# K's bias moved from a matmul to VectorE, and pieces of the order moved, in a fused attention and mixture-of-experts kernel on one core

## The chip, the core and the metric

The kernel runs on one NeuronCore of a Trainium2 chip. The core has TensorE (matmuls and transposes, which write into eight PSUM banks of 128 x 512 floats), VectorE, ScalarE and GpSimd (elementwise work), and SyncE, whose queue issues most of the DMAs. Each engine takes its instructions strictly in its own order; between engines only semaphores order the work. The metric is the device time of one execution in microseconds, lower is better.

## The reference, cut to what matters

For x of shape 2 x 1024 x 512, with a modulation (sa, ca, ga, sb, cb, gb) made from c:

```
h = layernorm(x) * (1 + ca) + sa
Xn = layernorm(h) * gamma + beta
Q, K, V = split(Xn @ W_in + b_in)
K, V = rotary(K), rotary(V)                  # first 256 of 512 columns
A = 0.5 * sum_over_tokens(K/|K| * V/|V|) + 0.5
x = x + ga * ((A * Q) @ W_out + b_out + h)
h = layernorm(x) * (1 + cb) + sb
scores = softmax(h @ gate_w); top 2 of 8 experts
routed = sum over the 2 experts: weight * (silu(h @ w_gate_e) * (h @ w_up_e)) @ w_down_e
shared = (silu(h @ sw_gate) * (h @ sw_up)) @ sw_down     # 704 inner columns
x = x + gb * (routed + shared)
```

## The kernel before, in words

All large products are made of three matmuls (`product3`): each float32 factor is split into a high part, rounded to the matmul's format (ScalarE copies it: the functions that end in `_hi`), and the rest (VectorE subtracts: `_lo`); high x high, high x rest and rest x high are summed in a bank. The 2048 tokens are 16 tiles of 128 (NT = 16, eight for each of the two rows of x). The order of each engine is written out by hand.

**First phase, K and V** (loop over t = 0 to 15). TensorE: K of tile t (`kv_matmul(t, 0)`, 12 matmuls and one that adds the bias row), transposes of tile t + 1, V of tile t, small pieces named in SLOT_A and SLOT_B (tables of cosines, q's transposes, the modulation "mod", the vector "a0"), and `weighted_sums(t - 1)`. The bias row is kept in two rows of `bk` and added by a matmul with a column of two ones, L1866. Banks 2 and 4 hold K, 3 and 5 V. ScalarE: `v_square(t - 1)`, `k_row(t)` (copies K into `ksb`), `tokens_hi(t + 1)`, `k_square(t)` (sum of squares), table reads, `normed(t + 2)`, and for t = 10 to 13 `scaled_q`. VectorE: `products(t - 1)` (L1174, L1175 and the rotary product L1187), `modulated(t + 2)` (L1138 to L1145), `tokens_lo(t + 1)` (L1149), `x_statistics(t + 3)` (L1120 to L1122), parts of `wo` for t = 8 and 9, `scaled_q_lo` for t = 10 to 13 (L1230). GpSimd makes the powers (L593, L598). K's tile t needs `tokens_lo(t)`; the transposes of t + 1 need `normed(t + 1)`.

**Middle.** `m_first`, `h_matmul` and `m_second` fold A into the output matrix (mw), `y_bias` and `y_bias_rows` make one bias row `bh` from bank 7, and `spread_mod(1)` brings the shift sb of the second norm to all partitions (`bc_s`).

**Second phase, y** (loop over t). TensorE: `y_matmul(t)`, a bias matmul L2165, `m_second`, parts of the gate's logits, `transposes2(t - 2)`, and after the tiles in Y_CHUNKS one chunk of the shared expert's gate and up for group 0 (a chunk is 128 of the 704 inner columns, a group four tiles; chunk n needs `s_mul` of chunk n - 1 because all chunks of this phase use banks 4 and 5). VectorE: `second_rows` (L1338), statistics, `residual_part`, `tokens2_lo` (L1357), `ffn_rows` (L1350, L1352), for t = 6 four `m_block_late` and four `m_block_lo_late`, and `s_mul` (L1365) and `s_lo` (L1373) of the chunks.

**Third phase, shared expert and slots.** For g = 0 to 3 `shared_gate_up(g)` and `shared_down(g)`: down tiles t take banks 6, 7, 0 in turn and in the last group 6, 7. VectorE scales and adds the rows (`shared_rows`, L1472 and L1474, which release the bank by `s_row`), counts the slots of the tokens (`row_entries`, `slots`, `entry_experts`), and builds 32 one-hot matrices, three at a time (`one_hots`), which TensorE sums in the order of `slot_sums`. `columns()` reads the sum, GpSimd then gathers the tokens of experts 0 and 1 (L667), and `turn_rows` transposes them in steps (0 to 4) at the places in TURN_AT, between the tiles of `shared_down(3)`.

**Fourth phase, experts.** Pairs of experts in a loop, TensorE full, gathers and scatters on GpSimd.

Of the kernel before, what the change touches and what calls it, by code (L numbers as in the profile page):

```python
# [23 lines left out]
P = 128  # L24
# [40 lines left out]
Y_CHUNKS = {6: 0, 9: 1, 12: 2, 14: 3}  # L65
# [8 lines left out]
def build(nc, X, W_in, b_in, W_out, b_out, gamma, beta, gate_w, w_gate, w_up, w_down,  # L74
# [10 lines left out]
    with ctx:  # L85
# [27 lines left out]
        with ExitStack() as a_phase:  # L113
# [10 lines left out]
            arow = al("arow", [P, B, ROT])  # L124
            bk = al("bk", [P, D], F32R)
# [166 lines left out]
        def s_down_bank(t):  # L292

            return bank[(6, 7, 0)[t % 3] if t < NT - GT else (6, 7)[t % 2]]
# [64 lines left out]
        TURN_AT = [(0, 0, 1), (0, NS - 1, 0), (0, NS - 1, 1), (1, 0, 2), (1, 0, 3)]  # L359
# [49 lines left out]
        def _(sp):  # L409
# [60 lines left out]
            sp.wait_ge(bias_mm, 2)  # L470
# [26 lines left out]
            sp.wait_ge(h32_ready, 1)  # L497
# [208 lines left out]
        def _(act):  # L706
# [18 lines left out]
            def bias_row_hi(i):  # L725

                act.wait_ge(bias_mm, i + 1)
                nc.scalar.activation((bk, bv)[i][:, :], bank[(W_BANK, MISC_BANK)[i]][:, :], ACT.Copy).then_inc(bias_hi, 1)
# [16 lines left out]
            def k_row(t):  # L745

                act.wait_ge(k_mm, t + 1)
                if t >= 2:
                    act.wait_ge(multiplied, t - 1)
                nc.scalar.activation(ksb[:, t % 2, :], bank[K_BANKS[t % 2]][:, :], ACT.Copy).then_inc(k_copied, 1)  # L750

            def k_square(t):
                if t:
                    act.wait_ge(v_sq, t)
                nc.scalar.activation(junk[:, :], bank[K_BANKS[t % 2]][:, :], ACT.Square,
                                     accum_out=nrm[:, t, 0:1]).then_inc(k_sq, 1)
# [57 lines left out]
            normed(1)  # L814
            bias_row_hi(1)
# [3 lines left out]
            for t in range(NT):  # L819
# [7 lines left out]
                k_row(t)  # L827
# [90 lines left out]
            for k in range(1, DC):  # L918
                scaled_q(1, k)
            m_block_hi(0, 3)  # L920
            shared_in_hi(0)
            act.wait_ge(h32_ready, 1)
            nc.scalar.activation(bh[:, :], junk[:, :], ACT.Copy).then_inc(bh_hi, 1)
            shared_in_hi(1)
# [4 lines left out]
            for t in range(NT):  # L929
# [9 lines left out]
                if t == NB - 2:  # L939
                    for i in range(DC):  # L940
                        m_block_hi_late(i)
                if t in Y_CHUNKS:
                    s_silu_of(0, Y_CHUNKS[t])
                if t - 1 in Y_CHUNKS:
                    s_hi_of(0, Y_CHUNKS[t - 1])

            def shared(g):
                for m in range((DC, 2, 0, 0)[g], NS):
# [3 lines left out]
                    if not g and m == DC:  # L952
                        tokens2_hi(NT - 2)
                        tokens2_hi(NT - 1)
                        shared_down_hi(0)
                s_hi_of(g, NS - 1)
                if not g:
                    read_parts(NG - 1)
                    shared_down_hi(1)
# [133 lines left out]
        def _(dve):  # L1093
# [64 lines left out]
            def bias_rows(i):  # L1158

                dve.wait_ge(bias_hi, i + 1)  # L1160
                dve.scalar_tensor_tensor((bk, bv)[i][:, :], (bk, bv)[i][:, :].bitcast(F32), nodd[:, :],
                                         bank[(W_BANK, MISC_BANK)[i]][:, :], ALU.mult, ALU.add).then_inc(bias_ready, 1)

# [89 lines left out]
            weights_lo(0)  # L1253
            tokens_lo(0)
# [7 lines left out]
            x_statistics(2)  # L1262
            for t in range(NT):
# [7 lines left out]
                if 1 <= t < NT - 1:  # L1271
                    tokens_lo(t + 1)
                if t + 3 < NT:
# [27 lines left out]
            def y_factors():  # L1301

                for b in range(B):
                    at = slice(b * Q4, (b + 1) * Q4)
                    dve.tensor_copy(comb_ga[at, :], bc_ga[at, b, :])
                    link(dve.tensor_tensor(comb_s[at, :], bc_s[at, b, :], bc_ga[at, b, :], ALU.mult))

            def y_bias():
# [3 lines left out]
                link(dve.tensor_tensor(junk[:, :], bank[H_BANK][:, :], bout[:, :], ALU.add))  # L1312
                link(dve.tensor_tensor(junk[0:half, :], junk[0:half, :], bank[H_BANK][half:P, :], ALU.add))
# [121 lines left out]
            def shared(g):  # L1435
                for m in range((DC, 2, 0, 0)[g], NS):
# [3 lines left out]
                    if not g and m == DC:  # L1440
                        tokens2_lo(NT - 2)
                        tokens2_lo(NT - 1)
                        shared_down_lo(0)
# [157 lines left out]
            def slots():  # L1601

                link(dve.scalar_tensor_tensor(flat(rr), flat(low), float(CAP - GN), flat(rr), ALU.mult, ALU.add))
# [193 lines left out]
        def _(pe):  # L1797
# [54 lines left out]
            def kv_matmul(t, i):  # L1852

                to = bank[(K_BANKS, V_BANKS)[i][t % 2]][:, :]
                if t >= 2:
                    pe.wait_ge((k_sq, v_sq)[i], t - 1)
                if i == 0:
                    pe.wait_ge(t_lo, t + 1)
                for k in range(DC):
                    if t == 0:  # L1860
                        pe.wait_ge(w_lo, DC * i + k + 1)
                    product3(to, [tokens(t, s)[:, k, :] for s in range(2)], [wkv[:, s, i, k, :] for s in range(2)],
                             k == 0, False)
                if t == 0:
                    pe.wait_ge(bias_ready, i + 1)
                nc.tensor.matmul(to, pairs4[:, :].to_broadcast([P, P]), (bk, bv)[i][:, :], start=False, stop=True)\  # L1866
                    .then_inc((k_mm, v_mm)[i], 1)

            def misc(name):
# [3 lines left out]
                if n < 2:  # L1873
                    pe.wait_ge(bias_ready, 2)
                else:
# [109 lines left out]
            for t in range(NT):  # L1985
                kv_matmul(t, 0)
                if t == 0:
                    bias_row(1)
# [9 lines left out]
            pe.wait_ge(k_sq, NT - 1)  # L1998
# [12 lines left out]
            def shared_gate_up(g, chunks=range(NS)):  # L2011
                for m in chunks:
# [24 lines left out]
                    if g == 2:  # L2037
                        slot_sums(m + 1)
                    if g == 3 and m < 2:
# [236 lines left out]
```

## Time and profile before

| | before |
|---|---|
| runs, median (lowest to highest) | 672.84 us (672.34 to 675.55), 3 runs |
| profiled execution, its own time | 675.52 us |
| its span, first to last instruction | 673.7 us |
| TensorE busy, mean granted clock | 645.6 us (96%), 0.991 |
| VectorE / ScalarE / GpSimd busy | 494.9 / 268.8 / 162.3 us |
| first phase, K of tile 1 to K of tile 15 | 31.3 to 150.1 us |
| second phase, y of tile 0 to y of tile 15 | 171.4 to 268.1 us |
| experts' first matmul | 446.1 us |

A row of a timeline gives the start, the duration, the engine, the line and operation, the tiles (written<-read) and, in brackets, how long the engine stood idle before and what released it. The records of matmuls overlap: the array takes up the next one while the end of the last is still on its way.

### The profile page before, as it was taken

What the parts mean: (1) busy time and instruction counts of PE and PEld (TensorE: products, weight loads), DVE (VectorE), ACT (ScalarE), POOL (GpSimd) and SP (SyncE); (2) the same over time, 40 slices, a digit from 0 to 9 for tenths busy, and PEclk for the clock granted to TensorE, in tenths of its full rate; (3) what the DMA queues carried; (4) which work ended last, traced back from release to release, by engine and by line L of the source; (5) the groups of instructions that cost most, each with busy time, mean ns of one, the idle gap of its engine ahead of it and who ended that gap; (6) DMA issues with size and microseconds to landing.
All of it is one profiled execution on the core that took longest, in us unless ns stands there. A gap on an engine that the chain in (4) does not pass through costs nothing.

```text
span 673.7 us, 10565 instructions
## 1 busy us (share of the span) xinstructions
PE 645.6 (96%) x3666; PEld 532.0 (79%) x3666; DVE 494.9 (73%) x1086; ACT 268.8 (40%) x525; POOL 162.3 (24%) x211
## 2 busy tenths in 40 slices
PE   7889999999998999999999999999999999999995
PEld 3567577777776787788778788789999899899994
DVE  4876789847699997457885784458778696886953
ACT  3454345444434442322101301426447364474530
POOL 1133233320011111100000003202654435453123
PEclk9989999999998999999999999999999999999998
DMA  8913031005234452513033035246777667666144
GB/s 331 400 35 111 18 110 32 31 17 173 73 130 140 145 192 79 156 48 110 0 112 100 1 119 167 71 133 207 119 177 195 109 194 129 173 185 106 48 60 62
DMA packets 41152, 80.81 MB, mean 120 GB/s; under 512 B 5020, under 2 KB 13230, under 8 KB 40567
## 3 DMA queue, kind: packets, MB, share of 16 engines
q1 hardware_dynamic: 33382, 62.06, 27.8%
q0 software_dynamic: 7728, 18.22, 14.5%
q8 instruction: 23, 0.38, 0.2%
q14 instruction: 19, 0.15, 0.1%
HBM read 58.88 MB, written 22.56 MB: 121 GB/s over the span
## 4 chain that ended last, share of the span: by engine, by line
PE 74%; DVE 14%; DMA 4%; issue 3%; ACT 2%; POOL 1%; SPq 1%; another core or an unknown queue 0%; POOLq 0%; DVEq 0%; ACTq 0%
PE bank L1800 20%; PE bank L1802 19%; PE bank L1801 19%; PE bank L2110 4%; PE bank L2087 2%; PE bank L1930 1%; DMA sdraw<-in_L_ffn_sw_down 1%; PE bank L2115 1%; PE bank L1848 1%; DVE st L1120 1%; PE bank L1866 1%; DVE sgu L1105 1%; DVE rows L1338 1%; DVE hx L1350 1%; DMA bc_s<-mod_d 1%
## 5 line engine op out<-in xcount | busy, mean ns | idle before, releaser
L1800 PE MATMUL bank<-ht,ew 128*128 128x256 f32 (+1 forms) x256 | 74.2, 290 | 0.0
L679 POOL DMA_INDIRECT out_rows<-y,si x35 | 54.8, 1564 | 78.5 <-DVE y L1730 69.0
L1801 PE MATMUL bank<-ht,ew 128*128 128x256 f32 (+1 forms) x256 | 73.1, 285 | 0.0
L1802 PE MATMUL bank<-ht,ew 128*128 128x256 f32 (+1 forms) x256 | 73.0, 285 | 0.0
L1800 PE MATMUL bank<-xt,sgu 128*128 128x512 f32 x176 | 69.5, 395 | 2.3 <-DVE bc_c L1365 1.4
L1802 PE MATMUL bank<-xt,sgu 128*128 128x512 f32 x176 | 68.6, 390 | 0.0
L1801 PE MATMUL bank<-xt,sgu 128*128 128x512 f32 x176 | 68.6, 390 | 0.0
L1800 PE MATMUL bank<-wkv,xt 128*128 128x512 f32 x128 | 54.6, 426 | 0.7 <-DVE xt L1149 0.7
L1801 PE MATMUL bank<-wkv,xt 128*128 128x512 f32 x128 | 50.7, 396 | 0.0
L1802 PE MATMUL bank<-wkv,xt 128*128 128x512 f32 x128 | 50.7, 396 | 0.0
L1801 PEld LDWEIGHTS bank<-ht,ew 128*128 128x128 f32 x256 | 48.2, 188 | 0.0
L1800 PEld LDWEIGHTS bank<-ht,ew 128*128 128x128 f32 x256 | 48.2, 188 | 0.0
L1802 PEld LDWEIGHTS bank<-ht,ew 128*128 128x128 f32 x256 | 48.2, 188 | 0.0
L667 POOL DMA_INDIRECT picked<-h_d,gi x36 | 41.9, 1163 | 22.9 <-issue 8.5
L659 POOL COPY gi<-gidx 128x5 int32 (+1 forms) x8 | 3.2, 397 | 170.0 <-DVEq L1639 130.7
L1800 PEld LDWEIGHTS bank<-xt,sgu 128*128 128x128 f32 x176 | 33.0, 188 | 9.7 <-DVE bc_c L1365 1.9
L610 POOL TENSOR_TENSOR rs<-ve,nhalf 128x1 f32<-128x1 f32 x16 | 15.4, 961 | 98.5 <-DVE ve L1122 98.5
L1802 PEld LDWEIGHTS bank<-xt,sgu 128*128 128x128 f32 x176 | 33.0, 188 | 7.1
L1800 PE MATMUL bank<-ew,gtR 128*128 128x512 f32 (+1 forms) x96 | 38.5, 401 | 0.1
L1801 PEld LDWEIGHTS bank<-xt,sgu 128*128 128x128 f32 x176 | 33.1, 188 | 6.3
L1802 PE MATMUL bank<-ew,gtR 128*128 128x512 f32 (+1 forms) x96 | 37.9, 395 | 0.0
L1801 PE MATMUL bank<-ew,gtR 128*128 128x512 f32 (+1 forms) x96 | 37.8, 394 | 0.0
(374 smaller groups left out, 1635.0 us busy)
## 6 DMA issues: line engine op xcount, KB each, us to landing
xring<-in_L_attn_X SPq DMA_DIRECT2D x32, 256.0 KB, 2.8
ewst<-in_L_ffn_w_gate SPq DMA_DIRECT2D x8, 704.0 KB
ewst<-in_L_ffn_w_up SPq DMA_DIRECT2D x8, 704.0 KB
slots<-in_L_wmod SPq DMA_DIRECT2D x4, 1024.0 KB, 7.3
x_d<-rows SPq DMA_DIRECT2D x16, 256.0 KB, 2.0
h_d<-hx SPq DMA_DIRECT2D x16, 256.0 KB, 2.0
xrow<-x_d SPq DMA_DIRECT2D x16, 256.0 KB, 2.7
out_rows<-xrow SPq DMA_DIRECT2D x16, 256.0 KB, 2.1
```

The source lines that it names most:

```text
L610: pool.tensor_tensor(rs[:, 2, t:t + 1], ve[:, 2, t:t + 1], nhalf[:, 0:1], ALU.pow).then_inc(rs3_ready, 1)
L667: pool.indirect_dma_start(out=picked[par][:, j, :], out_offset=None, in_=h2_d, in_offset=bass.IndirectOffsetOnAxis(ap=gi[:, par, j:j + 1], ...
L679: pool.indirect_dma_start(out=out, out_offset=bass.IndirectOffsetOnAxis(ap=si[0:CR[j], par, j:j + 1], axis=0), in_=y[0:CR[j], j, :], in_of ...
L1105: dve.tensor_tensor(sgu[:, 1, k, :], sgraw[:, k, :], sgu[:, 0, k, :].bitcast(F32), ALU.subtract)\
L1120: link(dve.bn_stats(st6[:, :], row))
L1338: dve.scalar_tensor_tensor(rows_of(t), u_of(t), mv1[:, t, 0:1], bank[Y_BANKS[t % 2]][:, :], ALU.add, ALU.add).then_inc(x2_ready, 1)
L1350: link(dve.scalar_tensor_tensor(hx_of(t), rows_of(t), mv2[:, t, 0:1], bc_cb[:, b, :], ALU.subtract, ALU.mult))
L1800: nc.tensor.matmul(dst, a[0], b[0], start=first, stop=False)
L1801: nc.tensor.matmul(dst, a[0], b[1], start=False, stop=False)
L1802: return nc.tensor.matmul(dst, a[1], b[0], start=False, stop=last)
L2087: last = nc.tensor.transpose(bank[RT_BANKS[(par + s) % 2]][:, i * P:(i + 1) * P], picked[par][:, j, k * P:(k + 1) * P], ident[:, :])
L2110: nc.tensor.matmul(bank[to[c % 2]][0:n, 0:width], packed[:, k, i * P:i * P + n], tok[part][:, k, :], start=k == 0 and not part, stop=k == ...
```

## The change

It does the following, and nothing else:

- K's bias: the matmul L1866 goes from all tiles of K. Once, after K of tile 0, `k_bias` spreads the row over all partitions in bank 6, and ScalarE copies it to a new tile `kb` (it lies where `bk` lies). `k_row` goes from ScalarE to VectorE, which adds `kb` as it takes K from its bank, after `tokens_lo(t + 1)`; `k_square` reads `ksb` and waits for it; the bank is free at `k_copied`.
- `x_statistics(2)` goes ahead of `tokens_lo(0)`.
- `spread_mod(1)` waits for `y_factors` in place of `y_bias`; in the middle the parts of `scaled_q(1, k)`, `m_block_lo(0, 3)` and `shared_in_hi(0)` go behind or into `y_bias`.
- Chunks of group 0 stand after tiles 6, 7, 10, 13 in place of 6, 9, 12, 14; ScalarE does `s_hi` of the last chunk ahead of `s_silu` of the next.
- The split of the down weights, first half, goes behind the silus of chunks 4 and 5.
- `row_entries` gives one gather to `slots`; `entry_experts` goes behind the first one-hots; slot parts 6 to 10 are built and summed at other places, `columns` one chunk later.
- The last four down tiles take banks 6, 7, 5, 4; the turns stand one place earlier.

```diff
-Y_CHUNKS = {6: 0, 9: 1, 12: 2, 14: 3}
+Y_CHUNKS = {6: 0, 7: 1, 10: 2, 13: 3}
...
-            return bank[(6, 7, 0)[t % 3] if t < NT - GT else (6, 7)[t % 2]]
+            return bank[(6, 7, 0)[t % 3] if t < NT - GT else (6, 7, 5, 4)[t - NT + GT]]
...
-        TURN_AT = [(0, 0, 1), (0, NS - 1, 0), (0, NS - 1, 1), (1, 0, 2), (1, 0, 3)]
+        TURN_AT = [(0, 0, 0), (0, 0, 1), (0, NS - 1, 0), (0, NS - 1, 1), (1, 0, 2)]
...
-            sp.wait_ge(h32_ready, 1)
+            sp.wait_ge(st_ready, 2)
             spread_mod(1, bc_sb, sb_in)
...
             def k_square(t):
                 if t:
                     act.wait_ge(v_sq, t)
-                nc.scalar.activation(junk[:, :], bank[K_BANKS[t % 2]][:, :], ACT.Square,
+                act.wait_ge(k_copied, t + 1)
+                nc.scalar.activation(junk[:, :], ksb[:, t % 2, :], ACT.Square,
                                      accum_out=nrm[:, t, 0:1]).then_inc(k_sq, 1)
...
             normed(1)
+            act.wait_ge(bias_mm, 2)
+            nc.scalar.activation(kb[:, :], bank[W_BANK][:, :], ACT.Copy).then_inc(bias_hi, 1)
             bias_row_hi(1)
...
-                k_row(t)
                 if 1 <= t < NT - 1:
                     tokens_hi(t + 1)
                 k_square(t)
...
-            for k in range(1, DC):
-                scaled_q(1, k)
+            scaled_q(1, 1)
             m_block_hi(0, 3)
-            shared_in_hi(0)
+            scaled_q(1, 2)
+            scaled_q(1, 3)
             act.wait_ge(h32_ready, 1)
             nc.scalar.activation(bh[:, :], junk[:, :], ACT.Copy).then_inc(bh_hi, 1)
+            shared_in_hi(0)
             shared_in_hi(1)
...
+                if t - 1 in Y_CHUNKS:
+                    s_hi_of(0, Y_CHUNKS[t - 1])
                 if t in Y_CHUNKS:
                     s_silu_of(0, Y_CHUNKS[t])
-                if t - 1 in Y_CHUNKS:
-                    s_hi_of(0, Y_CHUNKS[t - 1])
...
                         tokens2_hi(NT - 1)
-                        shared_down_hi(0)
                 s_hi_of(g, NS - 1)
                 if not g:
                     read_parts(NG - 1)
+                    shared_down_hi(0)
                     shared_down_hi(1)
...
+            def k_row(t):
+
+                dve.wait_ge(k_mm, t + 1)
+                if t == 0:
+                    dve.wait_ge(bias_hi, 2)
+                else:
+                    dve.wait_ge(multiplied, t)
+                if t >= 2:
+                    dve.wait_ge(k_sq, t - 1)
+                dve.tensor_tensor(ksb[:, t % 2, :], bank[K_BANKS[t % 2]][:, :], kb[:, :], ALU.add).then_inc(k_copied, 1)
...
             weights_lo(0)
+            x_statistics(2)
             tokens_lo(0)
...
-            x_statistics(2)
             for t in range(NT):
...
                     tokens_lo(t + 1)
+                k_row(t)
                 if t + 3 < NT:
                     x_statistics(t + 3)
...
                 link(dve.tensor_tensor(junk[:, :], bank[H_BANK][:, :], bout[:, :], ALU.add))
+                m_block_lo(0, 3)
...
-            for k in range(1, DC):
-                scaled_q_lo(1, k)
             m_block(0, 3)
-            m_block_lo(0, 3)
             dve.wait_ge(bout_in, 16)
             y_bias()
+            scaled_q_lo(1, 1)
             y_bias_rows()
+            scaled_q_lo(1, 2)
             residual_part(0)
+            scaled_q_lo(1, 3)
...
-                    if g == 2:
+                    if g == 2 and m < NS - 1:
                         one_hots(HOTS * (m + 2), HOTS)
-                    if g == 3 and m == 0:
-                        one_hots(HOTS * 10, HOTS)
-                    if g == 3 and m == 1:
+                    if g == 3 and m < 2:
+                        one_hots(HOTS * (9 + m), HOTS)
+                    if g == 3 and m == 2:
                         columns()
                 s_lo_of(g, NS - 1)
                 if not g:
+                    shared_down_lo(0)
                     shared_down_lo(1)
                 if g == 1:
                     slots()
-                    entry_experts()
...
-                for of, to in ((extra[:, 3, :], ahead), (order[:, 3, :], sl), (order[:, 2, :], low)):
+                for of, to in ((extra[:, 3, :], ahead), (order[:, 3, :], sl)):
...
             one_hots(0, HOTS)
+            entry_experts()
             shared_rows(1, (2, 3))
...
             shared_rows(2, (0, 1))
+            one_hots(HOTS * 7, HOTS)
+            shared_rows(2, (2, 3))
             one_hots(HOTS * 8, HOTS)
-            shared_rows(2, (2, 3))
-            one_hots(HOTS * 9, HOTS)
...
                 if t >= 2:
-                    pe.wait_ge((k_sq, v_sq)[i], t - 1)
+                    pe.wait_ge((k_copied, v_sq)[i], t - 1)
...
+                if i:
+                    if t == 0:
+                        pe.wait_ge(bias_ready, 2)
+                    last = nc.tensor.matmul(to, pairs4[:, :].to_broadcast([P, P]), bv[:, :], start=False, stop=True)
+                last.then_inc((k_mm, v_mm)[i], 1)
+
+            def k_bias():
+
+                pe.wait_ge(bias_ready, 1)
+                nc.tensor.matmul(bank[W_BANK][:, :], pairs4[:, :].to_broadcast([P, P]), bk[:, :],
+                                 start=True, stop=True).then_inc(bias_mm, 1)
...
-                                pe.wait_ge(s_row, t - 2 if t < NT - GT else t - 1)
+                                pe.wait_ge(s_row, min(t - 2, NT - GT) if t != NT - GT else t)
```

In TensorE's order `slot_sums` changes as `one_hots` does (parts 1 to 5 behind the first five chunks of group 2, parts 6 and 7 behind its down pairs, 8 to 10 behind the first three chunks of group 3), and the experts' second column block, not the first, waits for the last rows of the shared expert.

## Rows read from the trace of the kernel before

**Rows 1.** Timeline of TensorE, tile 9: start us, us, engine, line, operation, tiles.
```profile
113.63 0.39 PE L1802 MATMUL bank<-wkv,xt 128*128 128x512 f32 x1
113.86 0.39 PE L1866 MATMUL bank<-bk,pairs 128*128 128x512 f32 x1
114.09 0.60 PE L1848 MATMUL bank<-ident,hz 128*128 128x128 f32 x4
```
**Rows 2.** Who TensorE waited for, 174 to 230 us: total, times, longest.
```profile
PE bank L1800 <- DVE rows L1338: 2.0, 2, 1.5
```
**Rows 3.** Timeline of VectorE, the loop over tile 11.
```profile
118.29 0.68 DVE L1174 TENSOR_TENSOR prod<-bank,ksb 128x512 f32<-128x512 f32 x1
...
122.67 0.69 DVE L1149 TENSOR_TENSOR xt<-bank,xt 128x512 fp32r<-128x512 f32 x1
123.28 0.68 DVE L1120 BATCH_NORM_STATS2 st<-xring 128x6 f32<-128x512 f32 x1
...
125.06 0.75 DVE L1230 SCALAR_TENSOR_TENSOR swq<-wqT,a_col,swq 128x512 fp32r<-128x512 f32 x1 [0.69 <-ACT swq L796]
```
**Rows 4.** Timeline of VectorE, products at both ends of loop 9.
```profile
102.93 0.68 DVE L1174 TENSOR_TENSOR prod<-bank,ksb 128x512 f32<-128x512 f32 x1
...
110.17 0.68 DVE L1174 TENSOR_TENSOR prod<-bank,ksb 128x512 f32<-128x512 f32 x1
```
**Rows 5.** Timeline of ScalarE, the loop over tile 11.
```profile
122.52 0.60 ACT L755 ACTIVATE junk<-bank 128x512 f32<-128x512 f32 x1
...
123.60 0.82 ACT L735 ACTIVATE hz<-hz,nm,rs 128x512 f32<-128x512 f32 x1 [0.39 <-POOL nm L599]
```
**Rows 6.** Timeline of VectorE in the start.
```profile
29.56 0.69 DVE L1120 BATCH_NORM_STATS2 st<-xring 128x6 f32<-128x512 f32 x1
...
31.31 0.75 DVE L1138 SCALAR_TENSOR_TENSOR hz<-xring,mv,bc_c 128x512 f32<-128x512 f32 x1 [0.66 <-POOL rs L593]
```
**Rows 7.** Timeline of TensorE in the start.
```profile
35.84 0.66 PE L1848 MATMUL bank<-ident,hz 128*128 128x128 f32 x4 [1.32 <-ACT hz L735]
...
39.20 0.63 PE L1801 MATMUL bank<-wkv,xt 128*128 128x512 f32 x1
39.63 0.63 PE L1802 MATMUL bank<-wkv,xt 128*128 128x512 f32 x1
```
**Rows 8.** Windows: length, busy (instructions) of each engine, TensorE's granted clock, DMA.
```profile
36.90:38.50 1.60, 1.60 (x3) 0.84 (x3) 1.51 (x3) 1.60 (x5) 0.89 (x2) 0.51 0.01 5
...
100.00:120.00 20.00, 20.00 (x111) 15.00 (x110) 18.46 (x43) 10.23 (x24) 6.75 (x13) 1.00 0.10 27
```
**Rows 9.** Timelines of SyncE's queue and of VectorE, middle and second phase.
```profile
174.00 0.38 SPq L443 DMA_DIRECT2D bc_s<-mod_d  x1
...
179.41 0.75 DVE L1338 SCALAR_TENSOR_TENSOR rows<-u,mv,bank 128x512 f32<-128x512 f32 x1 [3.32 <-DMA bc_s<-mod_d]
...
221.74 0.67 DVE L1365 TENSOR_TENSOR ewst<-ewst,bank 128x512 f32<-128x512 f32 x1
```
**Rows 10.** Timeline of TensorE, matmuls behind a gap, second and third phase.
```profile
221.97 0.48 PE L1800 MATMUL bank<-mw,xt 128*128 128x512 f32 x1 [1.52 <-DVE mw L1298]
...
286.65 0.50 PE L1800 MATMUL bank<-xt,sgu 128*128 128x512 f32 x1 [1.45 <-DVE bc_c L1365]
...
330.80 0.50 PE L1800 MATMUL bank<-sd,gtS 128*128 128x512 f32 x1 [0.55 <-DVE gtS L1373]
...
340.25 0.50 PE L1800 MATMUL bank<-sd,gtS 128*128 128x512 f32 x1 [0.78 <-DVE xrow L1474]
...
379.98 0.40 PE L1800 MATMUL bank<-sd,gtS 128*128 128x512 f32 x1
```
**Rows 11.** Timeline of TensorE, the last down tiles.
```profile
436.91 0.50 PE L1800 MATMUL bank<-sd,gtS 128*128 128x512 f32 x1 [0.67 <-DVE xrow L1474]
```
**Rows 12.** DMA issues: count, KB each, median us to landing.
```profile
h_d<-hx SPq DMA_DIRECT2D x16, 256.0 KB, 2.0
```
**Rows 13.** Loads of x tiles, 0 to 60 us, and their landing.
```profile
DMA to landing us min/median/max: 2.7/5.4/12.9
```

More of the change, by code:

```diff
@@ L124, in build @@
             arow = al("arow", [P, B, ROT])
+            with ExitStack() as row_phase:
+                kb = region(row_phase)("kb", [P, D])
             bk = al("bk", [P, D], F32R)
@@ L469, in _ @@
             sp.wait_ge(w_lo, 2 * DC)
-            sp.wait_ge(bias_mm, 2)
+            sp.wait_ge(bias_mm, 3)
             load_mod(0)
@@ L725, in bias_row_hi @@
             def bias_row_hi(i):
-                act.wait_ge(bias_mm, i + 1)
+                act.wait_ge(bias_mm, 2 * i + 1)
                 nc.scalar.activation((bk, bv)[i][:, :], bank[(W_BANK, MISC_BANK)[i]][:, :], ACT.Copy).then_inc(bias_hi, 1)
@@ L743, in tokens_hi @@
                 nc.scalar.activation(tokens(t, 0), chunked(bank[T_BANKS[t % 2]][:, :]), ACT.Copy).then_inc(t_hi, 1)
[L745 to L750, printed above, removed]
             def k_square(t):
@@ L1158, in bias_rows @@
             def bias_rows(i):
-                dve.wait_ge(bias_hi, i + 1)
+                dve.wait_ge(bias_hi, 2 * i + 1)
                 dve.scalar_tensor_tensor((bk, bv)[i][:, :], (bk, bv)[i][:, :].bitcast(F32), nodd[:, :],
                                          bank[(W_BANK, MISC_BANK)[i]][:, :], ALU.mult, ALU.add).then_inc(bias_ready, 1)
+            def k_row(t):
[7 more added lines that the diff above has]
+                dve.tensor_tensor(ksb[:, t % 2, :], bank[K_BANKS[t % 2]][:, :], kb[:, :], ALU.add).then_inc(k_copied, 1)
             def products(t):
@@ L1305, in y_factors @@
                     dve.tensor_copy(comb_ga[at, :], bc_ga[at, b, :])
-                    link(dve.tensor_tensor(comb_s[at, :], bc_s[at, b, :], bc_ga[at, b, :], ALU.mult))
+                    last = dve.tensor_tensor(comb_s[at, :], bc_s[at, b, :], bc_ga[at, b, :], ALU.mult)
+                last.then_inc(st_ready, 1)
+                dve.wait_ge(st_ready, 2)
             def y_bias():
@@ L1442, in shared @@
                         tokens2_lo(NT - 1)
-                        shared_down_lo(0)
                     if g == 1 and m < NS - 1:
@@ L1596, in row_entries @@
             def row_entries():
-                for of, to in ((extra[:, 3, :], ahead), (order[:, 3, :], sl), (order[:, 2, :], low)):
+                for of, to in ((extra[:, 3, :], ahead), (order[:, 3, :], sl)):
                     gathered(of.unsqueeze(1).unsqueeze(1).to_broadcast(pair_e), to)
             def slots():
+                gathered(order[:, 2, :].unsqueeze(1).unsqueeze(1).to_broadcast(pair_e), low)
                 link(dve.scalar_tensor_tensor(flat(rr), flat(low), float(CAP - GN), flat(rr), ALU.mult, ALU.add))
@@ L1861, in kv_matmul @@
                         pe.wait_ge(w_lo, DC * i + k + 1)
[L1862 to L1867, printed above, removed]
+                    last = product3(to, [tokens(t, s)[:, k, :] for s in range(2)], [wkv[:, s, i, k, :] for s in range(2)],
+                                    k == 0, i == 0 and k == DC - 1)
+                if i:
[7 more added lines that the diff above has]
+                                 start=True, stop=True).then_inc(bias_mm, 1)
             def misc(name):
@@ L1874, in misc @@
                     pe.wait_ge(bias_ready, 2)
+                    pe.wait_ge(bias_hi, 2)
                 else:
@@ L1987, in _ @@
                 if t == 0:
+                    k_bias()
                     bias_row(1)
@@ L1997, in _ @@
                     weighted_sums(t - 1)
-            pe.wait_ge(k_sq, NT - 1)
+            pe.wait_ge(k_copied, NT)
             pe.wait_ge(v_sq, NT - 1)
@@ L2036, in shared_gate_up @@
                     last.then_inc(s_gu_mm, 1)
-                    if g == 2:
+                    if g == 2 and m < NS - 1:
                         slot_sums(m + 1)
-                    if g == 3 and m < 2:
-                        slot_sums(9 + m)
+                    if g == 3 and m < 3:
+                        slot_sums(8 + m)
             def slot_sums(part):
@@ L2073, in shared_down @@
                     if g == 1 and pair or g == 2:
-                        slot_sums(7 + pair if g == 2 else 0)
+                        slot_sums(NS + pair if g == 2 else 0)
             def turn_rows(w, par, steps):
@@ L2102, in expert_gate_up @@
                         pe.wait_ge(r_mul, 2 * NR * u + max(c - 1, 0) + 1)
+                    if c == 1:
+                        pe.wait_ge(s_row, NT)
                     tok = [ht[par][:, s, :, at] for s in range(2)]
@@ L2111, in expert_gate_up @@
                                                      start=k == 0 and not part, stop=k == DC - 1 and not part)
-                        pe.wait_ge(s_row, NT)
+                        pe.wait_ge(s_row, NT - 2)
                         pe.wait_ge(y_ready, CT * u + 1)
```

## The prediction

> **What bounds the kernel now.** I read the page's busy times first: TensorE is busy for 645.6 of 673.7 us and VectorE for 494.9. That figure alone is no bound, because the records of neighbouring matmuls overlap. The timeline of TensorE shows how to count: three 512-column matmuls and the transposes behind them start 0.23 us apart, though each record lasts 0.39 us [rows 1]. So a matmul taken out of a full stream is worth 0.233 us, not 0.39, and a gap before a matmul is its start, less the start before it, less 0.233. The Trainium skill says the same of busy time (Trainium Kernel Development and Optimization, Performance Expectations: matmul busy time is a bad metric because matmuls are pipelined). Next I read who TensorE waits for. The list is short and names VectorE nearly everywhere, the rows of the second phase first among its waits behind the start [rows 2]; TensorE's idle time is some 28 us in all, start and end included (673.7 - 645.6). So only three things can shorten the kernel: matmuls that go, those waits, and stretches at the lower clock. The timelines at each wait say what is late there.
>
> **K's bias: what TensorE saves.** The change takes the L1866 matmul from all 16 K tiles and puts one back (k_bias). For tiles 2 to 15 that is 14 x 0.233 = **-3.26 us** [rows 1]; tiles 0 and 1 are in the start, below. The skill's TensorE: Matmul & The Clock Gate ("Wait — 56ns, not 53.3ns?") gives 215.7 ns from start to start at 512 columns; by it the saving would be 3.02 us. The rows decide.
>
> **K's bias: what VectorE and ScalarE pay.** VectorE's new k_row reads a bank and SBUF like the product at L1174, 0.69 us, 0.61 to the next start; ScalarE loses its copy of 0.60. Both bounds are near: 0.61 and 0.69. VectorE's loop over a tile (products, modulated, tokens_lo, x_statistics) is 6.05 us without extras; in the loop that starts at 118.29, tokens_lo starts at +4.38, x_statistics at +4.99 and scaled_q_lo at +6.77, after a 0.69 us wait for ScalarE [rows 3]. TensorE's tile will be 7.25 - 0.23 = 7.02. With k_row a plain loop is 6.66 and stays ahead. Two kinds of loop don't:
> - Loops 8 and 9 carry two parts of wo (1.2 us). Loop 9 is 110.17 - 102.93 = 7.24 without idle [rows 4]; now it is 7.85. Loop 8, which begins level and meets a short wait for tokens_hi (0.1), leaves VectorE 0.9 us behind, loop 9 another 0.8.
> - Loops 10 to 13 carry scaled_q_lo, which waits for ScalarE's scaled_q, which stands behind normed. Until now ScalarE squared K right after its own copies, at 122.52, and normed, at 123.60, waited for GpSimd only [rows 5]. In the new order k_square waits for k_row, which VectorE does after tokens_lo: k_row at +4.99 to +5.68, the square 5.78, normed 6.39 (0.61 later), scaled_q 7.11, done 7.82, scaled_q_lo 7.85, next loop +8.52. So these loops take 8.5 us against 7.02 of TensorE (loop 10 with the a0 vector 9.2 against 7.7).
> VectorE thus stands 1.7 us behind at loop 10 and 3.1 at loop 11. TensorE needs tokens_lo of the next tile, which ends at +5.07 of a loop without backlog, only at +7.43 (K of tile 12 at 125.47 less 0.23, less the 117.81 at which V of tile 10 is there): 2.4 us of cover. Beyond it K of tile 12 starts 0.8 us late, and tiles 13 and 14 a further 1.5 each: **+3.8 us**. From tile 14 on VectorE has no modulated and catches up. The bounds of this term are 0 (the order hides it after all) and +5 (two more tiles at this pace).
>
> **The start.** x_statistics(2) leaves the place at 29.56, from which VectorE goes into modulated(2) at 31.31 after a wait for GpSimd [rows 6]; it fills the 0.94 us before tokens_lo(0), 0.1 more. kb's copy on ScalarE puts bias_row_hi(1) and thus VectorE's bias row 0.5 us later, of which 0.3 reaches the table product. Modulated(2) then starts at 29.85, 1.46 earlier; but normed(2) now stands behind k_square(0) and gains 1.1. TensorE waits for it at 35.84, then for the tables, and its clock falls to the lower level, 1.2 GHz: 0.51 of full from 36.9 to 40.4, where matmuls start 0.43 apart [rows 7, 8]. **-1.1 us**, and with half of the idle time gone I take the clock to stay up: **-1.4 us** (0.9 at the first matmul of V, 0.5 in the next three). Bounds 0 and -1.4.
>
> **Mod's spread and y_bias.** Before, spread_mod(1) waits for h32_ready: issued at 174.00, 5.3 us, so that VectorE starts second_rows(0) at 179.41 after 3.3 us of idle [rows 9]. From there to the last late M block VectorE is never idle, but for 0.45 twice, and TensorE waits for it. Now the load hangs on y_factors, done at 160, behind twelve weight loads issued till 161: it lands before 170. What is late next is VectorE's own queue: three scaled_q_lo leave the front (2.0 us), m_block_lo(0,3) fills the wait inside y_bias, h32 is ready 1.5 us earlier, and second_rows(0) follows scaled_q_lo(1,3) at 175.9: 3.5 us earlier. The chunk of gate and up that now stands at tile 7 waits for s_mul(0), VectorE's last piece of tile 6, at 222.34 - 3.54; TensorE resumes at 218.95 in place of 221.97 [rows 9, 10]: **-3.0 us**. The chunk at tile 13 puts y(14) behind it, so second_rows(14) starts 4.5 us before y(15) is there and takes 5.1 with s_lo: **+0.7 us** at the end of the phase.
>
> **shared_down_hi(0)** stood on ScalarE ahead of s_silu(0,5) and held it until the down weights had landed; TensorE resumed at 286.65 where 285.05 was due [rows 10]. Now silu goes first: **-1.6 us**. The down weights' split is done 2.6 us before it is needed.
>
> **Slots.** One gather (0.9 us) leaves the place ahead of s_mul(1,5) and s_lo(1,4): TensorE's start at 330.80, due 330.08: **-0.7**. entry_experts (2.8 us) leaves the place ahead of shared_rows(4): 340.25, due 339.32: **-0.9**. It goes between one_hots(0) and shared_rows(6), whose end moves but not beyond the stores, so slot part 1 waits 0.6 us, not 1.2: **-0.6**. Part 6 was summed as soon as it was made, three matmuls that hold TensorE from 378.00 to 379.98 (0.34 us when ready); it now has the first pair of down to hide in, though s_lo(2,4) is then 0.3 late: **-1.3** [rows 10]. Columns move behind the third chunk of group 3: cols_ready from 411.7 to 417.4, last gather issued at 424.9 and not 419.2, the first turn wanted at 430.2. Queue walk: nothing else waits on GpSimd, and SP's loads of expert 0 come after store 7 in any case.
>
> **Last turns and banks.** Four banks free t = 14 from its wait (436.91, 0.9 late [rows 11]), and turn 4 gets a whole tile to land, where the experts' first matmul waited 0.4, its rest matmul 0.4. But turn 3 moves ahead of t = 14 and needs picked_lo(1), which VectorE does behind shared_rows(12): a new wait of 1.5 us at 435.6. Sum **-0.95 us**.
>
> **Sum.** -3.26 + 3.8 - 1.1 - 1.4 - 3.0 + 0.7 - 1.6 - 0.7 - 0.9 - 0.6 - 1.3 - 0.95 = -10.3 us. The experts' loop from 446 on is untouched and moves as a whole. The profiled execution took 675.52 us (span 673.7), so its like is 665.2; the median of the runs shown is 672.84, which gives **662.5 us**, -1.5%.
>
> **Rivals.**
> - *The backlog costs nothing.* If VectorE and ScalarE keep pace in loops 10 to 13, the sum is -14.1: 658.7 us. For it: before, TensorE never waited there and VectorE was busy 18.5 of 20 us between 100 and 120 [rows 8]. Against it: the order of k_square and normed. Chance 0.2.
> - *Less of the gain arrives.* The clock stays low in the start (1.4 lost), and late gathers: nearest landings are 2.0 us for such a tile (h_d) and 12.9 us under full load [rows 12, 13]; with the latter the first turn waits 6.7 us. Some of that, 2 to 5 us: 664.5 to 667.5. Chance 0.22.
> - *No change that can be measured*, -3.3 us or less: both the gathers at 12.9 us and the backlog. 669.5 and over. Chance 0.08.
> - *Slower: the gaps of the backlog drop TensorE's clock.* At the lower level 25 matmuls a tile cost 0.19 more each, and sums and transposes 0.9: a tile of 12.7 us, 4.2 over VectorE's 8.5. Tiles 12 to 15 at it give +17, net +6.6: 679.4 us; it passes the old time from 2.5 such tiles and is slower by 0.5% from 3.3. Against it: behind gaps of 1.5 us at 221.97 and 286.65 the granted clock stayed at full, and the two falls seen last 3.5 us each. Chance 0.04.
>
> The likeliest has 0.46, with a range of its own of 660 to 665. For 8 in 10 the range goes from 657.5 (no backlog, a little more) to 668. A measurement of this kernel tells 0.5% (3.4 us) from no change; faster than that 0.87, within it 0.09, slower 0.04.
>
> **What would show it.** In the profile after: no L1866 on K but one; K's of tiles 13 and 14 with starts 8.5 us apart and idle TensorE before them, released by xt; the first second_rows 3 to 4 us after the bias row and no DMA wait; a wait for s_mul before the chunk at tile 7; none at 286 or for hot columns of part 6; a wait for ht before turn 3. The prediction is wrong if the K tiles run 7.0 apart to the end (then 658.7), or if the first turn waits for the gathers.

## The result, and the profile after

The changed kernel takes **670.26 us** (median of 8 runs, 668.52 to 671.15), the kernel before 673.42 (8 runs, 671.94 to 675.55) on the same chip. The ratio is 0.995 with a 95% interval of 0.9931 to 0.9968: 2.2 to 4.6 us less, 3.2 by the medians, where 10.3 less were forecast (662.5). The direction was right, and two thirds of the gain are missing.

The profiled execution has a span of 668.4 us against 673.7. Before asking why, I located the miss. For each matmul that both traces hold, I subtracted its start before from its start after; the table shows by how much this shift grows between the borders of my terms.

| from ... to (times of the kernel before) | forecast | measured |
|---|---|---|
| start ... V of tile 2 (47.95) | -2.7 | +0.7 |
| ... K of tile 15 (147.21) | +0.8 | +2.0 |
| ... chunk 4, end of y (269.21) | -2.3 | -2.2 |
| ... down of group 0 (300.08) | -1.6 | -1.7 |
| ... down of group 3 (426.75), the slots | -3.5 | -3.5 |
| ... second expert column block (449.25) | -0.95 | -0.7 |
| ... last matmul (665.64) | 0 | +0.6 |
| ... end of the span | 0 | -0.5 |

(K's bias is split over the first two rows, 0.23 and 3.03; 0.1 of the first row is a later start of this execution.) In the trace 5.0 of the 10.3 us are missing, and 4.6 of them in the first 150 us, the phase with K and V. The other 2.1 lie between the profiled execution of before and its median (below). The +0.6 behind the experts' second block is one wait:
```profile
466.02 0.50 PE L1814 MATMUL bank<-ew,gtR 128*128 128x512 f32 x1 [0.63 <-DVE y L1743]
```
Of the eleven variants below that have a part of the change, one more (all_three) shows it; so it belongs to the execution. The time from the last matmul to the end is 7.4 to 8.1 us in all the traces, which covers the -0.5.

Three rows of TensorE's waits in the first phase are new or longer. The list of who TensorE waited for, after (us in total, times, longest):
```profile
PE bank L1814 <- DVE xt L1147: 3.5, 4, 1.1
...
PE bank L1843 <- ACT bc_s L767: 1.8, 1, 1.8
...
PE bank L1910 <- ACT slots L769: 0.8, 1, 0.8
```
The first row holds the backlog that I forecast, 2.7 us in three waits; its fourth, 0.7 in the start, was there before. The other two are copies on ScalarE, and no step of mine has them. The 1.8 us one, in the timelines of ScalarE, VectorE and TensorE after:
```profile
36.27 0.60 ACT L745 ACTIVATE xt<-bank 128x512 fp32r<-128x512 f32 x1
40.53 0.63 ACT L751 ACTIVATE junk<-ksb 128x512 f32<-128x512 f32 x1 [3.67 <-DVE ksb L1171]
41.07 0.18 ACT L751 ACTIVATION_READ_ACCUMULATOR junk<-ksb 128x1 f32 x1
41.16 0.58 ACT L767 ACTIVATE bc_s<-bank 128x512 f32<-128x512 f32 x1
```
```profile
39.16 0.68 DVE L1147 TENSOR_TENSOR xt<-bank,xt 128x512 fp32r<-128x512 f32 x1
39.76 0.68 DVE L1171 TENSOR_TENSOR ksb<-bank,kb 128x512 f32<-128x512 f32 x1
```
```profile
41.79 1.12 PE L1843 MATMUL bank<-mrow,rowsel 128*128 128x512 f32 x2 [1.78 <-ACT bc_s L767]
```
ScalarE is idle for 3.67 us in front of k_square(1), which waits for VectorE's k_row(1). The copy of bc_s (read_misc) stands behind it. Its data has been there for most of that time (misc_first, below, shows it), and it frees the bank that TensorE's next table product needs. TensorE stands still for 1.78 us; the windows after (columns as in [rows 8]) show what follows:
```profile
41.80:43.40 1.60, 1.60 (x10) 0.44 (x10) 1.57 (x4) 1.33 (x3) 0.40 (x2) 0.98 0.00 0
43.40:46.50 3.10, 3.10 (x11) 2.48 (x8) 2.83 (x7) 0.00 (x0) 1.01 (x3) 0.50 0.00 0
```
The clock is at the lower level, 1.2 GHz, from 43.4 to 46.5. It had stayed up from 36.9 to 40.4, as forecast against [rows 7, 8]; a fall came 6.5 us later, behind the new wait. At 87.91 the same pattern makes TensorE wait 0.83 us more:
```profile
86.65 0.63 ACT L751 ACTIVATE junk<-ksb 128x512 f32<-128x512 f32 x1 [3.15 <-DVE ksb L1171]
...
87.28 0.58 ACT L769 ACTIVATE slots<-bank 128x512 f32<-128x512 f32 x1
```
```profile
87.91 0.74 PE L1910 MATMUL bank<-rowsel,slots 128*128 128x1 f32 x5 [0.83 <-ACT slots L769]
```
The backlog looks like its forecast. TensorE's first matmuls of K in tiles 12 to 14, and ScalarE's and VectorE's part between the first two:
```profile
126.02 0.47 PE L1814 MATMUL bank<-wkv,xt 128*128 128x512 f32 x1 [0.54 <-DVE xt L1147]
...
134.45 0.48 PE L1814 MATMUL bank<-wkv,xt 128*128 128x512 f32 x1 [1.10 <-DVE xt L1147]
...
142.87 0.47 PE L1814 MATMUL bank<-wkv,xt 128*128 128x512 f32 x1 [1.10 <-DVE xt L1147]
```
```profile
126.56 0.63 ACT L751 ACTIVATE junk<-ksb 128x512 f32<-128x512 f32 x1 [3.36 <-DVE ksb L1171]
...
127.20 0.80 ACT L737 ACTIVATE hz<-hz,nm,rs 128x512 f32<-128x512 f32 x1
127.90 0.71 ACT L792 ACTIVATE swq<-wqT,a_col 128x512 fp32r<-128x512 f32 x1
```
```profile
125.79 0.68 DVE L1171 TENSOR_TENSOR ksb<-bank,kb 128x512 f32<-128x512 f32 x1
...
128.65 0.75 DVE L1239 SCALAR_TENSOR_TENSOR swq<-wqT,a_col,swq 128x512 fp32r<-128x512 f32 x1 [1.17 <-ACT swq L792]
```
K tiles 8.4 us apart where 7.0 was due; VectorE idle for 1.17 us at the end of the chain k_row, k_square, normed, scaled_q. Compare [rows 3, 5].

From there on the other terms are in the trace. TensorE's matmuls behind a gap, answering to [rows 10] and, in the last line, to [rows 11]:
```profile
221.66 0.50 PE L1814 MATMUL bank<-xt,sgu 128*128 128x512 f32 x1 [0.46 <-DVE ewst L1378]
...
269.65 0.47 PE L1814 MATMUL bank<-xt,sgu 128*128 128x512 f32 x1 [1.14 <-DVE rows L1351]
...
348.19 0.38 PE L2069 MATMUL bank<-hot_col,hot_row 128*128 128x240 f32 x1 [0.44 <-DVE hot_col L1445]
...
432.50 0.33 PE L2110 MATMUL bank<-ident,picked 128*128 128x128 f32 x1 [1.21 <-DVE ht L1679]
```
The chunk at tile 7 starts at 221.66; less the 2.67 us by which this phase began late that is 218.99, forecast 218.95. No wait is left at 286, 330 and 340, and turn 3 waits 1.21 (forecast 1.5).

### The profile page after: what moved, and what is told of

Same layout as the page of the kernel before. It is cut to its first block, busy times and chain, and to the rows that moved or that the text cites. A ratio compares the mean times of both kernels' runs of the same rounds, so it can differ in the third digit from the quotient of the medians.

```text
span 668.4 us, 10563 instructions
## 1 busy us (share of the span) xinstructions
PE 640.5 (96%) x3651; PEld 529.4 (79%) x3651; DVE 504.2 (75%) x1102; ACT 262.2 (39%) x510; POOL 163.9 (25%) x211
## 4 chain that ended last, share of the span: by engine, by line
PE 71%; DVE 18%; issue 4%; ACT 3%; DMA 1%; POOL 1%; SPq 1%; another core or an unknown queue 0%; POOLq 0%; ACTq 0%; DVEq 0%
PE bank L1814 19%; PE bank L1816 19%; PE bank L1815 19%; PE bank L2135 4%; PE bank L2110 2%; DVE hz L1139 1%; DVE hz L1136 1%; DVE st L1140 1%; PE bank L2140 1%; DVE xt L1147 1%; DMA xring<-in_L_attn_X 1%; PE bank L1952 1%; DVE st L1118 1%; DVE srow L1484 1%; PE bank L2198 1%
## 5 line engine op out<-in xcount | busy, mean ns | idle before, releaser
L661 POOL COPY gi<-gidx 128x5 int32 (+1 forms) x8 | 4.6, 573 | 169.8 <-DVEq L1652 130.6
```

## The experiments

The question is whether K's part failed through ScalarE's order, which an edit of the order alone can mend, or because VectorE has no time for k_row. Times are medians; "before" is the kernel before on the same chip in the same rounds. Its median moves between 672.0 and 673.4 from set to set, so that a difference to the changed kernel has two readings, by the medians and by the ratios to before (times 673); where they differ I give both. For runs that touch the phase with K and V I also give its length in the trace, from the first matmul of K to K of tile 15: 126.2 us before, 128.8 in the changed kernel.

**misc_first.** On ScalarE only:
```
+                for name in SLOT_A.get(t, ()):
+                    read_misc(name)
                 k_square(t)
-                for name in SLOT_A.get(t, ()):
-                    read_misc(name)
```


> Theory (ScalarE's queue): in the changed kernel ScalarE's copies of table and query results (read_misc) stand behind k_square, and k_square now waits for VectorE's k_row. TensorE waits for such a copy at 41.79 (1.78 us), after which its clock falls (matmuls 0.43 apart for three us, 1.3 us lost), and again at 87.91 (0.83 us). With read_misc ahead of k_square both waits go: 2.6 us less, 3.9 if the clock stays up, so 666.4 to 667.7 beside 670.3; the K waits of tiles 12 to 14 (3.4 us) stay. Rival (VectorE is short of time, whatever ScalarE's order): VectorE's 0.61 us of k_row a tile is the bound, both waits come back elsewhere, 670 within 0.7.

Measured: 665.59 us (before 672.03), ratio 0.9898, interval 0.9872 to 0.9925. That is less than the changed kernel by 4.7 us (medians, 0.8 beyond the range expected) or 3.5 (ratios); the phase takes 123.9 us, 4.9 less. ScalarE after the edit, and TensorE's clock:
```profile
36.86 0.60 ACT L745 ACTIVATE xt<-bank 128x512 fp32r<-128x512 f32 x1
37.61 0.60 ACT L767 ACTIVATE bc_s<-bank 128x512 f32<-128x512 f32 x1 [0.15 <-PE bank L1843]
41.12 0.63 ACT L751 ACTIVATE junk<-ksb 128x512 f32<-128x512 f32 x1 [2.91 <-DVE ksb L1171]
```
```profile
41.00:47.00 6.00, 6.00 (x36) 4.39 (x35) 5.76 (x15) 3.20 (x7) 1.63 (x3) 1.00 0.00 0
```
The copy runs 3.5 us earlier, though this execution began 0.6 later. K_square still waits (2.91 us), but no copy stands behind it. Both TensorE waits are gone and the clock stays at 1.00 in the whole phase, which is 2.4 us shorter than before; my forecast for it was -2.0, with a backlog of 3.8 that measured 3.4. So the terms of this phase hold together once the copies are out of the way.

**square_last_late.** k_square behind normed, wo's parts and scaled_q, in loops from 9 on.

> k_square goes behind normed and scaled_q on ScalarE, from tile 9 on only. Theory (ScalarE's queue): the K tiles at 126.02, 134.45 and 142.87 of the changed kernel are 8.4 us apart because VectorE's scaled_q_lo waits for scaled_q, which stands behind k_square, which waits for k_row. With k_square last the loop is VectorE's own work, 6.05 + 0.61 + 0.61 = 7.27 against TensorE's 7.02, and the lag of 1.7 from the two parts of wo stays: the waits before K fall from 3.4 us to about 0.3, so 667.0 to 667.6 beside 670.3. Rival (VectorE itself is short of time): K tiles stay over 8 us apart, 670 within 0.7.

Measured: 667.15 (before 672.03), ratio 0.9924, 0.9896 to 0.9952: 3.1 less (medians) or 1.7 (ratios); the phase takes 125.9 us, 2.9 less. The K tiles of 12 to 14 start at 125.60, 132.68 and 140.12: 7.1 and 7.4 apart, not 8.4. This is in the range expected.

**square_last.** k_square at the end of every loop.

> k_square goes last in every loop on ScalarE, behind read_misc, normed, wo's parts and scaled_q. Theory (ScalarE's queue): both gains at once, 2.6 to 3.9 at the tables and 2.8 to 3.1 at the late K tiles, and normed(2) is 0.6 earlier in the start: 663.2 to 664.9 beside 670.3. Rival (VectorE is short of time): under 1.5 us of gain, 669 or more.

Measured: 662.94 (before 672.03), ratio 0.9849, 0.9822 to 0.9875: 7.3 less (medians) or 6.8 (ratios), 0.3 below the expected range. By the medians the two gains add up (4.7 + 3.1 against 7.3). In the traces the phase takes 122.2 us, 6.6 less, not 7.8: this execution had a fall of the clock at 21 us that the others did not, of which more below. The earlier normed(2) that I expected brings nothing: TensorE's wait behind it, for the copy of the table cs at 37 us, grows from 0.40 to 1.00. ScalarE in the loop over tile 11, and TensorE's one wait before a late K that is left:
```profile
121.70 0.82 ACT L737 ACTIVATE hz<-hz,nm,rs 128x512 f32<-128x512 f32 x1 [2.71 <-POOL nm L601]
122.42 0.71 ACT L792 ACTIVATE swq<-wqT,a_col 128x512 fp32r<-128x512 f32 x1
123.03 0.61 ACT L751 ACTIVATE junk<-ksb 128x512 f32<-128x512 f32 x1
```
```profile
136.40 0.47 PE L1814 MATMUL bank<-wkv,xt 128*128 128x512 f32 x1 [0.38 <-DVE xt L1147]
```
VectorE does all of its k_rows here too, so the rival (no time on VectorE) falls.

**no_k_part.** The changed kernel with K's bias matmul and ScalarE's k_row restored.

> The changed kernel with K's bias back on TensorE and ScalarE's own copy of K; all other parts of the change stay. Theory (K's part is what failed, all other steps came as forecast): from the end of the phase with K and V on, the changed kernel gains 8.0 us on the kernel before in the two traces, and the earlier x_statistics(2) gives 0 to 2.5 us more in the start: 662.9 to 665.4 beside 673.4 and 670.3. Rival (the later parts owe their gain to what K's part shifted, or the start costs by itself): 667 or more.

Measured: 664.39 (before 672.03), ratio 0.9884, 0.9858 to 0.991. The other parts alone are worth 7.8 us by the ratio, of which 3.4 are left in the changed kernel: K's part takes 4.4 away again (5.9 by the medians). The time is in the range expected.

**k_part_alone.** The kernel before with K's part and nothing else.

> The kernel before with K's part alone: bias added by VectorE, one bias matmul for K, k_square reading k_row's sum; all else as before. Theory (K's part as placed costs more than its 3.26 us): the waits of 1.8 and 0.8 us for ScalarE's copies and of 3.4 us before the late K tiles come, and the end of the phase with K and V on is 1.5 to 4 us later than before: 674 to 677 beside 673. Rival (the loss comes from K's part together with the earlier x_statistics(2) or other parts): 670 to 672.5.

Measured: 678.17 (before 673.02), ratio 1.0075, 1.0054 to 1.0095. That is 1.2 us beyond the range: K's part as placed costs 5.0 us. Its waits are the same three as in the changed kernel (the third, for slots, is 0.8 again). In the list of who TensorE waited for:
```profile
PE bank L1857 <- ACT hz L737: 4.0, 3, 1.9
PE bank L1809 <- DVE xt L1146: 3.5, 4, 1.1
...
PE bank L1838 <- ACT bc_s L767: 1.8, 1, 1.8
```
and one more that I had not priced: without the earlier x_statistics(2), normed(2) behind k_square(0) is late by 1.9 us where [rows 7] has 1.32.

**statistics_late.** The changed kernel with x_statistics(2) back at its old place.

> The changed kernel with x_statistics(2) behind the table product again. Theory (this part saves TensorE's wait for normed(2)): V(1) starts 1.0 to 2.0 us later, as in k_part_alone, and the following waits for ScalarE's copies move with it: 671.3 to 672.3 beside 670.3. Rival (the wait for the copy of bc_s hides it, as that copy hangs on VectorE's k_row(1)): 670.3 within 0.5.

Measured: 669.92 (before 672.65), ratio 0.9963, 0.995 to 0.9977: 0.3 less than the changed kernel by the medians, 0.9 more by the ratios, with intervals that overlap, so no difference that can be told. The rival holds. TensorE:
```profile
37.19 0.33 PE L1862 MATMUL bank<-ident,hz 128*128 128x128 f32 x1 [1.88 <-ACT hz L737]
...
44.18 0.70 PE L1843 MATMUL bank<-mrow,rowsel 128*128 128x512 f32 x1 [0.44 <-ACT bc_s L767]
```
Normed(2) is late again by 1.88, and in return the wait for the copy shrinks from 1.78 to 0.44. V of tile 2 starts at 49.51 in an execution that began 0.64 late, against 48.62. Each of the two traces has one fall of the clock up to there; in this one it lasts from 37.6 to 41.0 us and comes behind the wait for normed(2). In the changed kernel the earlier statistics thus buy nothing that can be measured; that they gain behind misc_first's open path is likely, but no run took them out there.

**spread_late.** The load of mod's second spread waits for h32_ready again (one line on SyncE).

> The changed kernel with the load of mod's second spread waiting for h32_ready again, as before; VectorE's new order stays. Theory (the early load is worth what I said): the load of 5.3 us starts when h32 is ready, 174.96, so VectorE's second_rows(0) starts at about 180.6 in place of 178.44, and TensorE resumes 2.2 us later at the chunk of tile 7: 672.4 beside 670.3. Rival (the y phase is bound elsewhere): 670.3 within 0.7.

Measured: 672.63 (before 673.02), ratio 0.9987, 0.9968 to 1.0006, about 2.4 more than the changed kernel, as the theory said. VectorE:
```profile
181.72 0.75 DVE L1351 SCALAR_TENSOR_TENSOR rows<-u,mv,bank 128x512 f32<-128x512 f32 x1 [1.61 <-DMA bc_s<-mod_d]
```
The DMA wait of [rows 9] is back at half its size. From K of tile 15 to chunk 4 this trace loses 1.5 us of the 3.0 that I gave to the whole edit, not the 2.2 expected. The rest I give to VectorE's new order, which no run tested alone. That this profiled execution is 2.4 us longer too has another cause in part: it has three falls of the clock, the changed kernel's has two.

**old_chunks.** The changed kernel with `Y_CHUNKS = {6: 0, 9: 1, 12: 2, 14: 3}`.

> The changed kernel with the chunks of gate and up behind tiles 6, 9, 12 and 14 again in place of 6, 7, 10 and 13. Theory (VectorE's queue sets the time from 178 to 222, wherever the chunks stand): y(8) waits for the late M blocks, ready at 221.0, where TensorE now resumes at 221.66, and the 0.76 us that the chunk at tile 13 costs at the end of the phase goes: 1.0 to 1.5 us less, 668.8 to 669.3. Rival (the chunk at tile 7 gives TensorE cover that it lacks at tile 9): 1 to 3 us more, 671.3 to 673.3.

Measured: 669.11 (before 673.02), ratio 0.9948, 0.9932 to 0.9964. The medians differ by 1.15 (in the range expected), the ratios by 0.1, so the whole times leave it open. The trace has the step: TensorE resumes at 221.07 in place of 221.66, and by 286 it is 1.3 us ahead.

**square_last_turns.** square_last with the last two turns one place later:
```
-        TURN_AT = [(0, 0, 0), (0, 0, 1), (0, NS - 1, 0), (0, NS - 1, 1), (1, 0, 2)]
+        TURN_AT = [(0, 0, 0), (0, 0, 1), (0, NS - 1, 0), (1, 0, 2), (1, 0, 3)]
```


> The kernel square_last with the last two of the five turns one place later (behind the first part of t = 14 and of t = 15), four banks kept. Theory (turn 3 waits 1.2 us for picked_lo(1), which VectorE does behind shared_rows(12)): that wait goes, and 0.2 to 0.4 us come back before the experts' first matmul: 0.8 to 1.0 us less than square_last, 662.0. Rival (the wait only moves to t = 14 or to the experts' first matmul): 662.9 within 0.4.

Measured: 661.91 (before 673.02), ratio 0.9844, 0.9821 to 0.9866. The wait of 1.2 us is gone from the trace; the median is 1.0 lower than square_last's, the ratio only 0.3 us; the whole times don't tell them apart.

**all_three.** The same with the old chunks.

> square_last_turns with the chunks of gate and up behind tiles 6, 9, 12 and 14. Theory (each of the three moves removes a wait of its own): the 1.2 us that old_chunks gained comes off square_last_turns too, 660.2 to 661.2. Rival (with TensorE earlier in the phase of y, its waits for VectorE's rows swallow it): 661.9 within 0.5.

Measured: **660.5** (before 672.67), ratio 0.9813, 0.9789 to 0.9836. The fastest version here: 1.9% less than before, and 9 to 10 us less than the changed kernel.

**before_again.** One more execution of the kernel before, with a profile.

> The kernel before once more, one execution with a profile. Theory (its executions differ by how often TensorE's clock falls): a time near 672 has one stretch at the lower clock fewer than the 675.5 of its first profile, or shorter ones, and the rest of the trace agrees within 0.5 us; a time near 675 has the same two. Rival: the difference lies in waits for transfers.

Measured: 674.05, span 672.3 (673.7 in the first profile). The theory missed: the two stretches at the lower clock are there and as long, and still the span is 1.4 us shorter. The rival holds: the difference is a transfer. ScalarE and TensorE:
```profile
281.02 1.49 ACT L716 ACTIVATE sd<-sdraw 128x1536 fp32r<-128x1536 f32 x1 [3.73 <-DMA sdraw<-in_L_ffn_sw_down]
```
```profile
285.08 0.50 PE L1800 MATMUL bank<-xt,sgu 128*128 128x512 f32 x1
```
ScalarE gets the down weights 1.6 us earlier than in the first profile (282.60), and the gap of 1.45 at 286.65 [rows 10] does not exist in this execution.

**down_early.** The changed kernel with the first half of the down weights split ahead of the silu again, as before.

> The changed kernel with the first half of the shared down weights split ahead of the silu again. Theory (the down weights land at another time in each execution, 281.0 in one of the kernel before and 282.6 in another, and TensorE waits at about 286 only when they land late): the median grows by 0 to 0.6 us, 670.3 to 670.9, and single executions are up to 1.6 longer. Rival (the stall of 1.57 us comes in most executions, as I read it in one): 671.8.

Measured: 669.5 (before 672.65), ratio 0.9952, 0.9933 to 0.997: 0.8 less than the changed kernel by the medians (below the range of the theory), 0.1 more by the ratios. Nothing is lost, against the rival's 1.6; the wait in its trace is 0.28 us.

## Why the prediction was wrong, by its own steps

- **K's bias, what TensorE saves** (-3.26): right. K tiles 8 and 9 start 7.01 us apart (96.52 and 103.53) against 7.26 before. The starts of neighbouring matmuls in [rows 1] are 0.23 apart, which is the price that I used. By the Trainium skill's figure of 215.7 ns (TensorE: Matmul & The Clock Gate, "Wait — 56ns, not 53.3ns?") I estimate 0.22 a tile; the starts in these rows decide for 0.23.
- **K's bias, what ScalarE pays: the step that failed.** I followed what stands behind the waiting k_square only through normed and scaled_q, and only in loops 10 to 13. Read_misc stands behind it too, in loops 1 and 6, and I had put nothing for it. Cost: 1.78 and 0.83 us of waiting, which delay TensorE's next K by 2.1 and 1.1 (measured against misc_first), and 1.5 for the clock that fell behind the first. The 1.5 is the time from K to V of tile 2 in the changed kernel, 5.19, less the 3.68 in old_chunks, which has the same wait and no fall there:
```profile
43.43 0.80 PE L1814 MATMUL bank<-wkv,xt 128*128 128x512 f32 x1
...
48.62 0.48 PE L1814 MATMUL bank<-wkv,xt 128*128 128x512 f32 x1
```
```profile
43.34 0.50 PE L1814 MATMUL bank<-wkv,xt 128*128 128x512 f32 x1
...
47.02 0.47 PE L1814 MATMUL bank<-wkv,xt 128*128 128x512 f32 x1
```
Together that is 4.7 of the 4.9 us that misc_first gives back in this phase.
- **The backlog** (+3.8): the K tiles come 0.60, 1.41 and 1.40 later than a pitch of 7.02, +3.4 in all. Square_last_late takes 2.9 of it away by ScalarE's order alone, as the step says. I called "the order hides it after all" a lower bound; no one had to hide it, an order without it was to be had.
- **The start** (-2.5): both facts came. Modulated(2) starts at 29.96 (29.85 forecast), the transposes at 34.80, 1.04 earlier (1.1), and the clock stayed up from 36.9 to 40.4. Then the wait for the copy and the fall behind it took it all: statistics_late shows the part without effect on the time. I had not followed the gain past the next wait.
- **Mod's spread and y_bias** (-3.0, +0.7): right, to 0.1 us in all. Second_rows(0) at 178.44 - 2.67 = 175.77 (175.9). Spread_late shows half of the 3.0 to be the load; old_chunks shows in the trace that the move of the chunks was no part of the gain but cost 1.3.
- **shared_down_hi(0)** (-1.6): right against that trace, wrong against the median. The stall is one of that execution: the trace of before_again has none, k_part_alone 0.21, down_early 0.28. The profiled execution of before was 2.1 us above the median of 673.42; this stall of 1.45 is most of it, and most of why the spans differ by 5.3 and the medians by 3.2. Subtracting a sum made on one execution from a median carried it over.
- **Slots** (-3.5): -3.45, gaps gone one by one as listed. Late gathers, the rival's mechanism, did not come: turn 0 runs at 425.46 without a wait.
- **Last turns** (-0.95): -0.7, with turn 3's wait of 1.21.

The result lies where I put "no change that can be measured" (8 in 100), but not by its mechanism. The slower rival's trigger did occur, a gap followed by the lower clock, but in the start and once, for 1.5 us. Its waits at K of 1.1 us let the clock stay up. As evidence against it I had named gaps of 1.5 us without a fall; I had missed that the second fall of the kernel before, at 204.2, comes with TensorE's wait of 1.54 us for VectorE's rows, which ends at 204.22.

One thing stays open: what K's part is worth when well placed. Square_last is 1.45 us under no_k_part by the medians, the intervals overlap, and in its trace a stretch at the lower clock (0.57 of full from 21 to 25) hides part of what TensorE saves. That stretch was in all three profiles of kernels with k_square last in every loop and in none of the others. The moved k_square can hardly be its trigger: in square_last the first one runs at 35.39, and TensorE's two waits ahead of the fall (1.83 and 0.74 us) are the same in the traces without it. Its cause stays open.

## What to carry to other kernels

When an operation moves to another engine, list everything that stands behind its consumer on the old engine, in every loop in which something stands there, and ask for each piece who waits for it; a consumer that now waits goes last in its loop. Follow an earlier start through to the next wait of the bounding engine before counting it. And of a stall that ends with a DMA, look at a second execution before it enters a sum that is taken from a median.

## What the runs showed of the hardware

TensorE's clock falls in stretches of the same length and not in the same number. Up to 650 us, every fall in the fourteen traces lasts 3.4 us at a granted clock of 0.5, which is 1.7 us lost. The profiled executions had none (no_k_part), one (misc_first, k_part_alone, down_early), two (most) or three (spread_late). The same kernel differs too: in the eight executions of square_last_late the mean granted clock goes from 0.996 to 0.985, and the two at 0.985 are the two slowest (670.1 and 670.63 us, against 664.62 for the fastest). Behind the same wait of 1.78 us for bc_s the clock fell in 2 of 6 traces (the changed kernel and spread_late), and behind the wait of 0.83 us at 88 in 4 of 7 (square_last_late, k_part_alone, spread_late, old_chunks). These traces are of different kernels with the same order around the wait. A short wait there had two prices: its own length and, in 6 of these 13 cases, a fall, which cost 1.5 us in the changed kernel.

The down weights were there for ScalarE 281.0 us into one execution of the kernel before and 282.6 into another, although the first of their loads was issued at nearly the same time (273.2 and 273.4). The slowest of the three loads took 6.7 us in the one and 8.1 in the other.
